# Dense stage of a fused attention and mixture-of-experts block: the last batch turned later, an expert's conversion moved, two scatters moved

## The reference

```python
router_logits = x @ gate_w.T                      # 16 experts
topk_w, topk_idx = top_k(softmax(router_logits), 4)
topk_w = topk_w / topk_w.sum(-1, keepdims=True)
combine = (one_hot(topk_idx, 16) * topk_w[..., None]).sum(1)
shared = (silu(x @ sg[:704].T) * (x @ sg[704:].T)) @ shared_down.T
shared = shared * sigmoid(x @ shared_gate_vec.T)
# for each of 16 experts, inner width 176:
acc = acc + (silu(x @ w_gate.T) * (x @ w_up.T)) @ w_d.T * cw[:, None]
return shared + acc
```

## Time and profile before

| | us |
|---|---|
| timed runs | 563.65, 561.6, 564.93 |
| median | 563.65 |
| the profiled execution's own time | 562.65 |
| its span | 560.9 |
| TensorE matmul busy | 516.0 (92%) |
| VectorE, ScalarE, POOL busy | 418.4 (75%), 343.8 (61%), 314.8 (56%) |
| mean granted TensorE clock | 0.985 |

### The profile page before, as it was taken

How to read it: one execution, slowest core, us unless ns; L and a number is a source line. 1 busy time by engine, 2 the same in 40 slices (tenths; PEclk the granted TensorE clock), 3 DMA queues, 4 the chain that set the end, 5 groups by cost and what they waited for, 6 DMA issues and landing times.

```text
span 560.9 us, 11857 instructions
## 1 busy us (share of the span) xinstructions
PE 516.0 (92%) x3614; PEld 395.7 (71%) x3614; DVE 418.4 (75%) x1065; ACT 343.8 (61%) x704; POOL 314.8 (56%) x342
## 2 busy tenths in 40 slices
PE   8977979999999999888989999989999999999992
PEld 3844445646564645345878888879999899999882
DVE  4978868887878785768864764757888876666876
ACT  3442766687669665776645345547887776666552
POOL 4832642583257321532377777715767688877663
PEclk9988999999999999999999999989999999999997
DMA  8551762445144524061024643658999988888983
GB/s 304 165 151 59 220 191 65 132 140 173 53 122 151 174 78 151 2 209 57 12 80 142 241 148 111 225 180 222 215 246 233 203 144 134 152 131 171 273 227 157
DMA packets 67916, 87.54 MB, mean 156 GB/s; under 512 B 6608, under 2 KB 59408, under 8 KB 67856
## 3 DMA queue, kind: packets, MB, share of 16 engines
q1 hardware_dynamic: 53408, 67.48, 38.8%
q0 software_dynamic: 14016, 18.92, 18.3%
q10 hardware_dynamic: 432, 0.39, 0.2%
HBM read 35.25 MB, written 38.73 MB: 132 GB/s over the span
## 4 chain that ended last, share of the span: by engine, by line
PE 30%; DMA 9%; DVE 6%; POOL 3%; issue 2%; ACT 2%; SPq 1%; POOLq 0%; ACTq 0%; DVEq 0%
PE gate_ps L2219 8%; DMA acc_dram<-yout,row_of 7%; PE y_ps L2242 5%; PE y_ps L2190 5%; PE gate_ps L1095 4%; PE up_ps L1095 4%; PE m_ps L2139 2%; DMA added<-acc_dram 1%; DMA ring<-acc_dram 1%; PE up_ps L2230 1%; PE up_ps L2231 1%; POOL fmrs L1583 1%; POOL acc_dram L1619 1%; POOL total L1639 1%; PE m_ps L2107 1%
## 5 line engine op out<-in xcount | busy, mean ns | idle before, releaser
L1619 POOL DMA_INDIRECT acc_dram<-yout,row_of x76 | 117.9, 1552 | 53.1 <-ACT yout L1764 26.6
L816 DVE TENSOR_REDUCE nmax<-a_ps 128x2 f32<-128x768 f32 (+3 forms) x88 | 96.2, 1120 | 15.7 <-PE a_ps L984 15.3
L679 ACT ACTIVATE probs<-a_ps 128x1024 f32<-128x1024 f32 (+1 forms) x96 | 81.5, 883 | 30.9 <-PE a_ps L1009 26.1
L571 POOL TENSOR_SCALAR_AFFINE_SELECT probs<-probs 128x256 f32<-128x256 f32 (+1 forms) x96 | 47.2, 501 | 87.8 <-ACT probs L679 87.6
L2219 PE MATMUL gate_ps<-w_all,rxT_hi 128*128 x316 | 77.5, 327 | 1.7 <-DVE rxT_lo L1974 0.9
L1607 POOL DMA_INDIRECT xs_dram<-xrow,idx x64 | 66.7, 1042 | 20.1 <-issue 16.7
L2242 PE MATMUL y_ps<-w_all,hT_hi 128*128 x237 | 57.2, 310 | 0.7 <-DVE hT_lo L2024 0.7
L979 PE MATMUL a_ps<-KTt,QT 96*128 96x128 bf16 (+3 forms) x256 | 50.7, 309 | 5.9 <-ACT probs L679 1.8
L2012 DVE TENSOR_TENSOR h<-rsilu,gate_ps 128x176 f32<-128x176 f32 x79 | 26.5, 335 | 37.4 <-ACT rsilu L1749 36.9
L2219 PEld LDWEIGHTS gate_ps<-w_all,rxT_hi 128*128 128x128 f32 x316 | 51.8, 188 | 3.4 <-issue 2.7
L1009 PE MATMUL a_ps<-QT,KTt 99*128 99x512 bf16 (+3 forms) x256 | 47.9, 301 | 4.7 <-DVE nmax L816 1.7
(11 more groups left out here) (345 smaller groups left out, 1368.9 us busy)
## 6 DMA issues: line engine op xcount, KB each, us to landing
xin<-xs_dram SPq DMA_DIRECT2D x79, 136.5 KB, 3.5
xs_dram<-zeros SPq DMA_DIRECT2D x7, 1365.0 KB, 7.1
w_all<-in_wex_dram SPq DMA_DIRECT2D x16, 480.0 KB, 4.1
KTt<-parts SPq DMA_DIRECT2D x42, 128.0 KB
QT<-parts SPq DMA_DIRECT2D x39, 128.0 KB
acc_dram<-zeros SPq DMA_DIRECT2D x6, 640.0 KB, 8.1
ring<-acc_dram SPq DMA_DIRECT2D x18, 128.0 KB, 3.9
acc_dram<-yst SPq DMA_DIRECT2D x4, 512.0 KB, 2.6
```

What stands on the lines that cost most here:

```text
L571: pool.affine_select(out=pr, in_=pr, pattern=[[0, nh], [1, P]], compare_op=ALU.is_ge, fill=0.0, base=0, channel_multiplier=-1).then_inc(ma ...
L679: nc.scalar.activation(dst, src, ACT.Exp, scale=float(DH) ** -0.5).then_inc(a_act, 1)
L816: nc.vector.tensor_reduce(nmax[:, i, h:h + nh].rearrange("p (b h) -> p b h", h=hb), src, AX.X, ALU.max, negate=True).then_inc(a_dve, 1)
L1619: pool.indirect_dma_start(out=acc[a][:, :], out_offset=bass.IndirectOffsetOnAxis(ap=row_of[:, p:p + 1].bitcast(mybir.dt.uint32), axis=0), ...
```

## The change

It edits constants and the order of work in four engines' loops. The turn of the last batch stays in step 4 (now `LATE_X - 1`) but stands behind `gate_up(5)` on TensorE. Its halves are made in step 5. The router product stands behind the down product of step 5, and `gate_up(6)`, the first product that reads the new `x2T`, behind the router product. The turn of the logits, the exponentials and the first routing piece come one step later; VectorE's expert order goes ahead of `hidden(6)`, ScalarE's `logT` copy ahead of `activate(6)`. The conversions of experts 0 to 3 stay at steps 18 to 21, there is none at step 22, and expert 4 comes at step 23 (`experts_at`). POOL's norms stand ahead of scatters 2 and 5, and the pace starts two events lower. The number of instructions of each kind is the same.

```diff
--- before.py
+++ after.py
@@ -33,7 +33,7 @@
 XROW = D + E + 1
 XIN, YOUT, ACCS = 12, 6, 3
 PACE = 2
-PACE_FROM = 2
+PACE_FROM = 0
 TAILS = 3
 WARM, KEEP, BRIDGE, BRIDGE_IN = 22, 3, 8, 4
 SPLIT = 4
@@ -1432,9 +1432,16 @@
 
         NSTEP = B * SH
 
-        LATE_X = 4
-        TURN_L, RANK1, TABLE = 5, 10, 14
-        NORM_AT = (0, 3)
+        LATE_X = 5
+
+        def experts_at(n):
+            if n == NSTEP - 2:
+                return ()
+            first = n - EXPERT0 - (n == NSTEP - 1)
+            return range(max(first, 0), min(n - EXPERT0 + 1, early))
+
+        TURN_L, RANK1, TABLE = 6, 10, 14
+        NORM_AT = (2, 5)
         NEXT_X = {LATE_X: 1, 9: 2, 16: 3}
 
         block = ctx.enter_context(nc.Block())
@@ -1719,21 +1726,21 @@
                     shared_out(n // SH - 1, range(TB))
                 if n in NEXT_X:
                     x2_high(NEXT_X[n])
+                if n == LATE_X:
+
+                    act.wait_ge(logT_ready, 1)
+                    nc.scalar.copy(logT[:], m_ps[:, 0, :]).then_inc(logT_copied, 1)
                 if n + 1 < NSTEP:
                     activate(n + 1)
                 if n + 3 < SH:
                     shared_high(n + 3)
                 if n in (1, 3):
                     late_rows(n // 2)
-                if n == LATE_X:
-
-                    act.wait_ge(logT_ready, 1)
-                    nc.scalar.copy(logT[:], m_ps[:, 0, :]).then_inc(logT_copied, 1)
                 if n == TURN_L + 1:
                     exponentials(nc, act, t, 1)
-                if 0 <= n - EXPERT0 < early:
-                    expert_high(n - EXPERT0)
-                    expert_tail_high(n - EXPERT0)
+                for k in experts_at(n):
+                    expert_high(k)
+                    expert_tail_high(k)
             rows_high(0)
             rows_high(1)
             shared_out(B - 1, range(0, TB // 2))
@@ -1915,7 +1922,7 @@
             hidden(0)
             shared_low(2)
             combining_last = combination(nc, t, link, 1)
-            plan = {1: [mixing], 4: [ordering], 5: [routing_last], 7: [routing_last, routing_last], 8: [routing_last, routing_last],
+            plan = {1: [mixing], 6: [routing_last], 7: [routing_last, routing_last], 8: [routing_last, routing_last],
                     9: [routing_last, combining_last], 10: [slots1], 11: [slots1, slots1], 12: [slots1], 13: [tabling],
                     14: [tabling]}
             for n in range(NSTEP):
@@ -1929,6 +1936,8 @@
                     next(mixing)
                 if n in NEXT_X:
                     x2_low(NEXT_X[n])
+                if n == LATE_X:
+                    next(ordering)
                 if n + 1 < NSTEP:
                     hidden(n + 1)
                 if n + 3 < SH:
@@ -1941,9 +1950,9 @@
                     dve.wait_ge(logit_ready, 1)
                 for piece in plan.get(n, ()):
                     next(piece)
-                if 0 <= n - EXPERT0 < early:
-                    expert_low(n - EXPERT0)
-                    expert_tail_low(n - EXPERT0)
+                for k in experts_at(n):
+                    expert_low(k)
+                    expert_tail_low(k)
 
 
             def add_first(i):
@@ -2143,27 +2152,21 @@
             gate_up(0)
             for n in range(NSTEP):
                 i, j = n // SH, n % SH
-                if n in NEXT_X:
-                    if n == LATE_X:
-                        pe.wait_ge(fm_normed, 1)
-                        pe.wait_ge(x2_lo, 1)
-                    else:
-
-                        pe.wait_ge(logit_ready, 1)
-                        pe.wait_ge(x2_lo, NEXT_X[n])
-                        if n > RANK1:
-                            pe.wait_ge(rank_read, 2)
-                            pe.wait_ge(tab_ready, 1)
+                if n in NEXT_X and n != LATE_X:
+
+                    pe.wait_ge(logit_ready, 1)
+                    pe.wait_ge(x2_lo, NEXT_X[n])
+                    if n > RANK1:
+                        pe.wait_ge(rank_read, 2)
+                        pe.wait_ge(tab_ready, 1)
                     turn_x2(NEXT_X[n])
-                if n + 1 < NSTEP:
+                if n + 1 < NSTEP and n != LATE_X:
                     gate_up(n + 1)
-                if n == LATE_X:
-
-                    pe.wait_ge(x2_lo, 2)
-                    for c in range(KT):
-                        ins = products(nc, m_ps[:, 0, :], (t["gw_hi"][:, c, :], t["gw_lo"][:, c, :]),
-                                       (x2T_hi[:, 1, c, :], x2T_lo[:, 1, c, :]), c == 0, c == KT - 1)
-                    ins.then_inc(logT_ready, 1)
+                if n == LATE_X - 1:
+
+                    pe.wait_ge(fm_normed, 1)
+                    pe.wait_ge(x2_lo, 1)
+                    turn_x2(1)
                 if n == TURN_L:
                     pe.wait_ge(logT_copied, 1)
                     for s in range(TB):
@@ -2191,6 +2194,14 @@
                                                start=(j == 0 and m == 0 and s % 2 == 0), stop=(j == SH - 1 and m == 1),
                                                skip_group_check=True)
                 ins.then_inc(down_done, 1)
+                if n == LATE_X:
+
+                    pe.wait_ge(x2_lo, 2)
+                    for c in range(KT):
+                        ins = products(nc, m_ps[:, 0, :], (t["gw_hi"][:, c, :], t["gw_lo"][:, c, :]),
+                                       (x2T_hi[:, 1, c, :], x2T_lo[:, 1, c, :]), c == 0, c == KT - 1)
+                    ins.then_inc(logT_ready, 1)
+                    gate_up(n + 1)
             turn_in(0)
             turn_in(1)
             for n in range(BRIDGE_IN):
```

## The result

The changed kernel takes 560.08 us (median of 8, 559.06 to 560.92) against 563.77 for the kernel before (median of 8, 561.6 to 565.75) on the same chip: ratio 0.9936, 95% interval 0.9913 to 0.9959. That is 3.7 us faster, between 2.3 and 4.9; the forecast was 560.0. The profiled execution shown here took 560.92, the highest of its eight, with a span of 559.2.

What follows compares the result with a forecast made beforehand. Two nearly equal paths into the routed stage, TensorE's dense chain and POOL's scatters with page loads, were taken to bound it; shortening both starts the first expert product 3.2 us earlier: 563.2 - 3.2 = 560.0 us, range 557.2 to 563.0.

Steps and rivals of the forecast that it cites:

- Part 1: Last batch's turn and router product, moved later behind gate and down products: net 0.9 us won, range 0.4 to 1.3.
- wait of down(6) for y_copied: TensorE's down product of step 6 waits for four copies started behind hid_hi(6): 0.2 us charged.
- Part 2: Two POOL scatters ahead of the first norm, pace lowered: last scatter starts 2.55 us earlier, norm not delayed.
- My reading of the power's 1.83 us: POOL's power in the first norm: 0.9 us of its time is waiting for a VectorE difference beside it.
- Part 3: Fifth expert's conversion behind step 23: last dense down product starts 1.25 us earlier, at full clock taking 0.95 us.
- The sum: At the routed stage's entry, the first expert product starts 3.2 us earlier.
- the two paths: TensorE's last down product ends at 368.35 and POOL's page 0 lands at 368.4; before, 0.4 us apart.
- Carried to the end: Routed stage's order is unchanged and hangs on its start, so the whole 3.2 us reaches the end.
- rival of absorption: Routed stage, with DMA engines 0.99 busy from 400 to 440, swallows the gain: 0.8 left, 562.4 us; chance 0.14.
- the norm is pushed: Second early scatter ends after 274.3; dense chain and POOL lose 0.8 us: gain 2.4, time 560.8; chance 0.18.
- The clock did not fall: Judges the rival that TensorE's clock still falls in the last dense hole: gain 2.1, time 561.1; chance 0.09.
- slower rival: From 394 to 437, six accumulating-scatter rounds at 6.67 us each lose 4.3 us: time 564.3; chance 0.07.

Runs made afterwards that it cites:

- run without part 3: New kernel with all five expert conversions back at steps 18 to 22: ratio 1.0005 to the kernel before.
- late norm run: New kernel with PACE_FROM 2, so the two early scatters wait for the first down product and hold up the norm: 566.8 us, ratio 1.0050; on the disturbed chip 0.9996.
- shorter entry: New kernel with page 0 turned in the last hole, no idle matmuls, expert 4's conversion behind page 0: 559.88 us, ratio 0.9944.
- second execution: Unchanged new kernel, profiled in a second comparison on another chip: 558.56 us, ratio 0.9913 to the kernel before at 563.0.
- part 2 alone: Kernel before with only PACE_FROM 0 and the norms ahead of scatters 2 and 5: ratio 1.0015.
- bridge run: New kernel with 16 idle matmuls instead of 4 ahead of the first expert product: 561.45 us, ratio 0.9970; on the disturbed chip 0.9983.
- parts 2 and 3 alone: Two runs on the kernel before: only scatters ahead of the norm with the pace, ratio 1.0015; only the fifth expert behind step 23, ratio 0.9996.
- pairs 1 and 3 and 1 and 2: New kernel with scatters and pace as before, ratio 1.0024; new kernel with conversions at steps 18 to 22 as before, ratio 1.0005.
- Part 1 alone: Kernel before with only the turn and the router product moved, run on the disturbed chip: ratio 1.0009.
- pair 2 and 3: Kernel before with early scatters, pace and the fifth expert behind step 23, turn and router product unmoved, on the disturbed chip: ratio 0.9977.
- disturbed chip: Chip on which every kernel took some 17 us longer, in unexplained dense-stage waits; kernel before 580.75 us there.

## Why the prediction was right

**Part 1.** Forecast: router product 4.8 us behind the normalised rows, 0.9 won by the end. Measured: 4.83 (287.93 to 292.76), and silu(23) 0.90 earlier, 0.96 in the run without part 3. The holes left are 0.40 and 0.23 instead of 0.6 and 0.5; the wait of down(6) for y_copied cost 0.1 instead of 0.2.

**Part 2.** Forecast: no delay of the norm, by a margin of 0.4 us. The norm's first operation is 7.96 us behind the first gate product, 8.02 before. It is a close thing: POOL goes from the second scatter to the norm with 0.08 us between, and the VectorE difference starts 0.34 us after the norm's first operation does. Two misses cancelled here, which is luck: the first scatter started 0.3 us later than forecast and took 1.49 us instead of 1.7, the second ended 0.1 later than forecast. My reading of the power's 1.83 us, half of it waiting for that difference, is shown by the late norm run: where no difference runs beside it, it takes 1.05. What I had not seen is that POOL would win more than two scatters. I gave 2.55 us; it was 3.8 here and in the shorter entry, 2.6 to 2.9 in the other undisturbed runs with part 2 and an early norm. So 2.55 is the size that is sure, and the rest depends on where the scatters fall against VectorE's differences: the 64 scatters were busy 66.7 us before and 64.8 after, but 66.4 in the second execution of the same kernel. There, two scatters that begin inside a difference (299.76 and 309.19) took 1.43 and 1.38 us again.

**Part 3.** Forecast 1.25 and full clock; measured 1.22, with 0.93 us from the first to the last start of the eight matmuls against 1.66.

**The sum.** Forecast 3.2 us at the entry, measured 3.3: 0.90 + 1.22, 0.73 from the clock in the down product, 0.4 in turns and bridge. The forecast had the two paths meet. In this execution they do not: its loads took 2.5 us or more to land, so page 0 is there at about 101.3 and is turned at 102.46; TensorE's path decides by 1.2 us. In the second execution they do meet: the loads start at 100.09, a landing of 2.2 us gives 102.3, page 0 is turned at 102.37, and for page 1, the next load, TensorE's weight load waited 0.4 us. G is nearly the same in both (103.98 and 104.11). Before, the two paths were some 0.7 apart, not 0.4 (102.46 + 2.2 to 2.3 against 105.40).

**The time.** That 560.0 met 560.08 to a tenth is luck. The kernel before had 563.77, 0.6 above what I took for it, and the gain was 0.5 above the 3.2, with an interval of 2.3 to 4.9. The profiled execution was forecast at 559.45 and took 560.92.

**Carried to the end.** The forecast let the 3.2 pass whole. In this execution 3.4 us are there at page 0, 3.0 at page 32 and 1.9 at page 40, counted at ScalarE's silu of the page. Between the last two the chain of the new kernel runs mostly over VectorE (an expert's conversion and selections), that of the kernel before mostly over TensorE. This looks like the rival of absorption, but it is spread: from page 24 to page 40 the kernel before took 34.6 us, the new one 36.0 here and 34.0 in its second profile, the other runs 34.0 to 36.3. From the first expert product to the end of the span the fourteen profiled executions took 187.6 us (the kernel before) to 192.5 (part 2 alone), more spread than the whole gain. So no single profile shows what an edit at the entry is worth at the end. The medians, with 3.7 and 4.4 us, decide for the forecast, and the bridge run, with 2.1 put in and 2.9 found, agrees.

**The rivals.** That the norm is pushed did not happen. The late norm run, a far larger push of 3.3 us, lost 5.8 us at the entry and 8.2 in the median: once TensorE stands long enough for its clock to fall, a slip costs more than its length. The clock did not fall after 0.74 us. The slower rival (rounds of accumulating scatters) did not show in the medians.

How much of the 3.3 is sure: 1.1 of it is the clock, which behind the same hole fell at once or later, and once not at all. Against an execution of the kernel before in which it does not fall the entry would be 2.2 us shorter, against the one traced it is 3.3.

## What to carry to other kernels

Where two chains of nearly equal length meet at the entry of a stage, read both to the meeting point before pricing an edit of one: here parts 2 and 3 alone, and the pairs 1 and 3 and 1 and 2, measured as nothing in time, and the three together gave 3.7 us. (Part 1 alone and the pair 2 and 3 ran on the disturbed chip only; the pair may hold most of the gain.) Work may be put in front of a critical small operation only if its own release comes early enough; the same two scatters, released by a later event, turned the gain into a loss. A gap of TensorE costs more than its length when the clock falls behind it, so shorten the long gaps first. And compare medians: the part behind an edit can vary from one execution to the next by more than the edit is worth.

## What the runs showed of the hardware

- Behind an equal hole of 1.95 to 1.97 us, the granted clock fell at once (kernel before, 0.51), within the first microsecond (part 1 alone, 0.67, then 0.50), after a microsecond (0.50, parts 1 and 2) or not at all (1.00, part 2 alone). Holes of 0.70 to 1.05 in and behind the dense stage were followed by 1.00 in every undisturbed run; waits of 2.44 and 3.35 there were both followed by 0.50. But the length of the hole does not decide alone. On the disturbed chip the clock stayed at 1.00 for at least 1.8 us behind waits of 3.46 (part 1 alone, at 301.14) and 2.86 us (bridge run, at 368.26), and was at 0.50 behind one of 1.80 (part 1 alone, at 310.74).
- In these traces a scatter on POOL is lengthened if it begins well inside a VectorE difference of two SBUF operands, and hardly if it begins with it. Before, it began at 277.44, the difference at 277.33: 1.94 us. Scatters that begin 0.2 us into a difference of 0.69 took 1.35 to 1.38. After, both began at 277.67:

```profile
277.67 0.98 DVE L1913 TENSOR_TENSOR sw_lo<-raw_w,sw_hi 128x768 fp32r<-128x768 f32 x1
```

  The scatter took 1.08, the difference 0.98 instead of 0.95. The Trainium skill (SBUF — State Buffer, "Who interferes with whom") says that the order of issue decides who blocks. The scatter's side of it agrees with these rows. VectorE's side does not show: a difference that began 0.6 us into a scatter (the one at 310.75) took the usual 0.69 us, and the one above, begun with the scatter, lost 0.03. Its inference that such a difference does not hold descriptor generation is not borne out by the 1.94.
- From idx being ready to the start of the first scatter there were 1.1 us (270.39 to 271.47), and in the late norm run 1.0 from the end of the down product that released it (271.58 to 272.58), not the 0.65 taken from a scatter whose predecessor was a POOL operation.
